# Last depth tile of a down projection with its low rank product in the same rows, in four weight versions

## What is computed

```python
def lora_add(base, inp, A, B):
    Ab = A[layer_idx][lora_indices]
    Bb = B[layer_idx][lora_indices]
    t = jnp.einsum('bri,bni->bnr', Ab, inp)
    return base + jnp.einsum('bor,bnr->bno', Bb, t) * SCALE
gate = lora_add(jnp.einsum('bnh,fh->bnf', x, W_gate), x, A_gate, B_gate)
up = lora_add(jnp.einsum('bnh,fh->bnf', x, W_up), x, A_up, B_up)
act = jax.nn.silu(gate) * up
down = lora_add(jnp.einsum('bnf,hf->bnh', act, W_down), act, A_down, B_down)
```

## Time and profile before

| | |
|---|---|
| median of 3 runs | 403.99 us (403.94 to 404.26) |
| profiled execution, its own time | 405.77 us |
| its span, first to last instruction | 403.9 us |
| PE busy | 398.2 us, 99% of the span, 1981 matmuls |
| weight loads (PEld, beside the matmuls) | 332.0 us, 82% |
| DVE busy | 309.1 us, 77% |
| ACT busy | 240.5 us, 60% |
| granted TensorE clock | 1.0 of full speed throughout |

### The profile page before, as it was taken

How to read it: one execution, slowest core, us unless ns; L and a number is a source line. 1 busy time by engine, 2 the same in 40 slices (tenths; PEclk the granted TensorE clock), 3 DMA queues, 4 the chain that set the end, 5 groups by cost and what they waited for, 6 DMA issues and landing times.

```text
span 403.9 us, 5691 instructions
## 1 busy us (share of the span) xinstructions
PE 398.2 (99%) x1981; PEld 332.0 (82%) x1981; DVE 309.1 (77%) x467; ACT 240.5 (60%) x381; POOL 13.4 (3%) x17
## 2 busy tenths in 40 slices
PE   8999999999999999999999999999999999999996
PEld 5899888888888888888888888888888888888885
DVE  4689978586745556683599887978787869899993
ACT  4769876767674379922655555565646485484740
POOL 5400000000000200000000000000000000000000
PEclk9999999999999999999999999999999999999999
DMA  7630234411111430300101113222131125105112
GB/s 260 199 115 2 79 105 111 119 52 54 52 54 32 133 99 0 105 0 0 54 0 52 54 53 104 63 94 97 60 104 54 60 83 194 54 0 197 53 52 104
DMA packets 14237, 31.88 MB, mean 79 GB/s; under 512 B 2306, under 2 KB 4610, under 8 KB 14210
## 3 DMA queue, kind: packets, MB, share of 16 engines
q1 hardware_dynamic: 13632, 29.96, 23.0%
q10 hardware_dynamic: 578, 1.57, 1.0%
HBM read 29.43 MB, written 2.10 MB: 78 GB/s over the span
## 4 chain that ended last, share of the span: by engine, by line
PE 97%; DMA 1%; issue 0%; DVE 0%; DVEq 0%; SPq 0%
PE bank L1311 47%; PE bank L1618 17%; PE bank L1502 15%; PE bank L1420 5%; PE bank L1448 3%; PE bank L1467 3%; PE bank L1456 3%; PE bank L1321 2%; PE bank L1516 1%; DMA wraw<-w_in 1%; PE bank L1523 0%; PE bank L1530 0%; DVE act L930 0%; DVEq L49 0%; SPq L287 0%
## 5 line engine op out<-in xcount | busy, mean ns | idle before, releaser
L1311 PE MATMUL bank<-xs,ws 128*128 128x512 f32 x840 | 194.2, 390 | 0.0
L1311 PEld LDWEIGHTS bank<-xs,ws 128*128 128x128 f32 x840 | 156.6, 188 | 32.3 <-ACT bank L399 0.5
L1502 PE MATMUL bank<-xs,wdc 128*128 128x512 f32 x264 | 61.5, 390 | 0.0
L1502 PEld LDWEIGHTS bank<-xs,wdc 128*128 128x128 f32 x264 | 49.1, 188 | 10.2 <-DVE xs L848 0.2
L399 ACT ACTIVATE xs<-act 128x512 fp32r<-128x512 f32 x71 | 42.9, 624 | 21.2 <-DVE act L995 7.6
L848 DVE TENSOR_TENSOR xs<-act,xs 128x512 fp32r<-128x512 f32 x71 | 47.7, 687 | 3.6 <-ACT xs L399 3.0
L848 DVE TENSOR_TENSOR ws<-wraw,ws 128x256 fp32r<-128x256 f32 (+2 forms) x49 | 32.5, 672 | 14.3 <-ACT ws L399 14.3
L399 ACT ACTIVATE bank<-bank 128x512 f32<-128x512 f32 x30 | 17.4, 580 | 39.8 <-PE bank L1311 38.9
L1618 PE MATMUL bank<-xs,vs 128*128 128x512 f32 x168 | 38.2, 389 | 0.0
L1618 PEld LDWEIGHTS bank<-xs,vs 128*128 128x128 f32 x168 | 31.5, 188 | 6.5
L399 ACT ACTIVATE ws<-wraw 128x256 fp32r<-128x256 f32 (+2 forms) x47 | 28.6, 619 | 11.1 <-PE bank L1311 4.1
(11 more groups left out here) (122 smaller groups left out, 423.1 us busy)
## 6 DMA issues: line engine op xcount, KB each, us to landing
wraw<-wgu_in SPq DMA_DIRECT2D x22, 512.0 KB, 3.3
wdr<-vs_in SPq DMA_DIRECT2D x7, 512.0 KB, 3.4
wdr<-wd_in SPq DMA_DIRECT2D x11, 256.0 KB, 2.6
wraw<-vj_in SPq DMA_DIRECT2D x3, 896.0 KB, 5.3
xa<-xT_in SPq DMA_DIRECT2D x4, 256.0 KB, 4.7
wraw<-w_in SPq DMA_DIRECT2D x4, 256.0 KB, 4.9
xa<-xT_in ACTq DMA_DIRECT2D x2, 512.0 KB, 6.2
bgu_raw<-bgu_in SPq DMA_DIRECT2D x32, 32.0 KB, 1.9
```

Of the source, the lines that this page charges most:

```text
L1311: ins = mm(z[:, :], ws[:, j % 2, w, s, k * P:(k + 1) * P], xs[:, c, r, k, :], start=(start and k == 0 and s == 0 and r == 0), stop=(k == 1 ...
L1502: ins = mm(z[:, :], wd[:, s, h * P:(h + 1) * P], x[r], start=(start and s == 0 and r == 0), stop=False, skip_group_check=True)
```

## The change

The 32 empty rows of the last depth tile are put to use. The result of `t_c` is scaled directly into rows 96 to 127 of the activation's last tile (`place_td`), and the weight tile gets B in the same rows. Since B depends on the sample and the 32 rows hold two samples' ranks, the weight tile exists in four versions, one for each pair of samples: 96 rows of W_down, the same in all four, and 32 rows of B. SP loads all four whole (`raw10`), ahead of tiles 6 to 9. `hi_w10` and `lo_w10` split them; version 0 lies in `wdc`, where the last tile was, the others in free parts of `ws`. `last_c(t, h)` takes the place of `main_c(t, 10)` and `lora_c(t, h)`: for each pair of 256 columns three passes. `tsum`, `bdr`, `td`, `bd` and their zeroing by GpSimd go. The ring slot of tile 10 isn't counted by `s_use` any more but by the fourth y.

```diff
-            tsum = sb("tsum", [32, 2, CH], f32, way)
-            bdr = sb("bdr", [64, 2, H], f32, way)
+            raw10 = sb("last_wd_raw", [P, 4, H], f32, way)
...
-        bd = [flat[:, 4 * CH:6 * CH].rearrange("p (q n) -> p q n", q=2) for flat in ws_flat]
-        td = [flat[:, 6 * CH:7 * CH] for flat in ws_flat]
+        w10 = [[wdc[:, FC - 1, s, :] for s in range(2)]] + [
+            [flat[:, (4 + s) * CH:(5 + s) * CH] for s in range(2)] for flat in ws_flat] + [[flat[:, 6 * CH:7 * CH] for flat in ws_flat]]
...
             sp.wait_ge(s_c12f, S1 // 2)
+            for v in range(4):
+                sp.dma_start(raw10[0:CR, v, :], wd_in[FC - 1, 0:CR, :]).then_inc(s_w10_ld, 16)
             for b in range(B):
-                row = 32 * (b // 4) + RANK * (b % 2)
-                sp.dma_start(bdr[row:row + RANK, b % 4 // 2, :],
-                             bd_in[ds(which[b], 1)].rearrange("o r h -> (o r) h")).then_inc(s_bd_ld, 16)
-            for n in range(6, FC):
+                row = CR + RANK * (b % 2)
+                sp.dma_start(raw10[row:row + RANK, b // 2, :],
+                             bd_in[ds(which[b], 1)].rearrange("o r h -> (o r) h")).then_inc(s_w10_ld, 16)
+            for n in range(6, FC - 1):
                 load_wd(n)
             load_w(G1 + 2)
...
-            pool.wait_ge(s_ad_pad, 1)
-            pool.wait_ge(s_p4, S1)
-            for t in range(2):
-                nc.gpsimd.memset(v32(bd[t][KS:P, :, :]), 0.0).then_inc(s_pad_d, 1)
-                nc.gpsimd.memset(v32(td[t][KS:P, :]), 0.0).then_inc(s_pad_d, 1)
...
-                    eng.wait_ge(s_act_pad, 1)
+                    eng.wait_ge(s_td, 4 * t + 4)
...
-                if u >= 10:
-                    a.wait_ge(s_use, u - 9)
+                if u == 20:
+                    a.wait_ge(s_y, 4)
+                elif u >= 10:
+                    a.wait_ge(s_use, min(u - 9, 11))
...
-            def hi_bd():
-                a.wait_ge(s_bd_ld, 16 * B)
+            def hi_w10(v):
+                a.wait_ge(s_w10_ld, 16 * (4 + B))
                 a.wait_ge(s_p4, S1)
-                for t in range(2):
-                    raw = bdr[32 * t:32 * t + 32, :, :]
-                    copy(bd[t][32 * t:32 * t + 32, :, :], raw).then_inc(s_bdhi, 1)
-                    copy(bd[t][64:KS, :, :], raw).then_inc(s_bdhi, 1)
-
-            def td_scale(t):
+                copy(w10[v][0], raw10[:, v, :]).then_inc(s_w10hi, 1)
+
+            def place_td(t):
                 a.wait_ge(s_t, t + 1)
                 for b in range(4):
-                    copy(tsum[:, t, b * P:(b + 1) * P], T_BANK[t][32 * b:32 * b + 32, b * P:(b + 1) * P], LORA_SCALE
-                         ).then_inc(s_tsum, 1)
-
-            def td_hi(t):
-                a.wait_ge(s_tsum, 4 * t + 4)
-                copy(td[t][0:32, :], tsum[:, t, :]).then_inc(s_tdhi, 1)
-                copy(td[t][32:64, :], tsum[:, t, :]).then_inc(s_tdhi, 1)
+                    first = t * CH + b * P
+                    copy(act[CR:P, FC - 1, first:first + P], T_BANK[t][32 * b:32 * b + 32, b * P:(b + 1) * P], LORA_SCALE
+                         ).then_inc(s_td, 1)
...
-                td_scale(t)
-                td_hi(t)
-            hi_wd(FC - 1)
+                place_td(t)
+            for v in range(4):
+                hi_w10(v)
             hi_ac(10)
-            hi_bd()
...
-            def lo_bd():
-                for t in range(2):
-                    v.wait_ge(s_bdhi, 2 * t + 1)
-                    sub(bd[t][32 - 32 * t:64 - 32 * t, :, :], bdr[32 * t:32 * t + 32, :, :], bd[t][32 * t:32 * t + 32, :, :]
-                        ).then_inc(s_bdlo, 1)
-
-            def td_lo(t):
-                v.wait_ge(s_tdhi, 2 * t + 1)
-                v.wait_ge(s_tsum, 4 * t + 4)
-                sub(td[t][64:KS, :], tsum[:, t, :], td[t][0:32, :]).then_inc(s_tdlo, 1)
+            def lo_w10(i):
+                v.wait_ge(s_w10hi, i + 1)
+                sub(w10[i][1], raw10[:, i, :], w10[i][0]).then_inc(s_w10lo, 1)
...
-            td_lo(0)
-            td_lo(1)
-            lo_wd(FC - 1)
+            for i in range(4):
+                lo_w10(i)
             lo_ac(10)
-            lo_bd()
...
-            def lora_c(t, h):
+            def last_c(t, h):
                 for q in range(2):
                     half = slice(256 * q, 256 * q + 256)
-                    ins = mm(Y_BANK[t][h][:, half], bd[t][:, q, h * P:(h + 1) * P], td[t][:, half],
-                             start=False, stop=(q == 1), skip_group_check=True)
+                    for s, r in PASSES:
+                        ins = mm(Y_BANK[t][h][:, half], w10[2 * t + q][s][:, h * P:(h + 1) * P], slot_c(11 * t + 10, r)[:, half],
+                                 start=False, stop=(s == 1), skip_group_check=True)
                 return ins
...
-            pe.wait_ge(s_wdlo, FC)
-            main_c(0, 10).then_inc(s_use, 1)
-            pe.wait_ge(s_bdhi, 4)
-            pe.wait_ge(s_bdlo, 2)
-            pe.wait_ge(s_pad_d, 4)
-            pe.wait_ge(s_tdhi, 4)
-            pe.wait_ge(s_tdlo, 2)
+            pe.wait_ge(s_w10lo, 4)
             for h in range(4):
-                lora_c(0, h).then_inc(s_y, 1)
-            pe.wait_ge(s_tsum, 8)
+                last_c(0, h).then_inc(s_y, 1)
+            pe.wait_ge(s_td, 8)
...
-                main_c(1, 10, range(h, h + 1))
-                lora_c(1, h).then_inc(s_y, 1)
+                last_c(1, h).then_inc(s_y, 1)
```

More of the change, by code:

```diff
@@ L192, in product_end @@
         def product_end(p):
-            return 12 + KF * (p + 1)
+            return 11 + KF * (p + 1)
         def tiles_of(g):
@@ L207, in build @@
         s_maskr = sem("mask_repeated")
-        s_act_pad, s_pad, s_pad_d = sem("short_act_padding_zero"), sem("padding_zero"), sem("down_lora_padding_zero")
+        s_act_pad, s_pad, s_ad_pad = sem("short_act_padding_zero"), sem("padding_zero"), sem("ad_padding_zero")
         s_table = sem("table_touched")
@@ L215, in build @@
         s_wd_ld = [sem("wd_loaded_even"), sem("wd_loaded_odd")]
-        s_ad_ld, s_bd_ld = sem("ad_loaded"), sem("bd_loaded")
+        s_ad_ld, s_w10_ld = sem("ad_loaded"), sem("last_wd_loaded")
         s_xr_ld = [sem(f"xres_loaded_{i}") for i in range(4)]
@@ L237, in build @@
         s_wdhi, s_wdlo = sem("wd_hi"), sem("wd_lo")
-        s_ad, s_ad_pad, s_bdhi, s_bdlo = sem("ad_placed"), sem("ad_padding_zero"), sem("bd_hi"), sem("bd_lo")
+        s_ad, s_w10hi, s_w10lo = sem("ad_placed"), sem("last_wd_hi"), sem("last_wd_lo")
         s_ahi, s_alo, s_use = sem("act_hi"), sem("act_lo"), sem("act_used")
-        s_t, s_tsum, s_tdhi, s_tdlo = (sem(n) for n in ("td_projected", "td_scaled", "td_hi", "td_lo"))
+        s_t, s_td = sem("td_projected"), sem("td_placed")
         s_y, s_sq, s_sqd, s_acc, s_sqhi, s_sqlo, s_ev, s_nm = (sem(n) for n in (
@@ L328, in _ @@
             load_w(G1 + 3)
-            sp.wait_ge(s_wdlo, FC)
+            sp.wait_ge(s_wdlo, FC - 1)
             sp.wait_ge(s_acc, 5)
@@ L575, in hi_down @@
                 if i >= 14:
-                    a.wait_ge(s_use, 12 + i - 13)
+                    a.wait_ge(s_use, 11 + i - 13)
                 elif i % 2 == 0:
@@ L639, in square @@
                 elif t == 1:
-                    a.wait_ge(s_wdlo, FC)
+                    a.wait_ge(s_wdlo, FC - 1)
                 to = third if (t, h) == (1, 2) else sqr[:, min(h, 1), :]
@@ L655, in rsqrt @@
                     a.wait_ge(s_warm, 3)
-                    a.wait_ge(s_bdlo, 2)
+                    a.wait_ge(s_w10lo, 4)
                 else:
@@ L1055, in norm @@
                 else:
-                    v.wait_ge(s_bdlo, 2)
-                    v.wait_ge(s_bdhi, 4)
+                    v.wait_ge(s_w10lo, 4)
                 nc.vector.scalar_tensor_tensor(y, N_BANK[t][:, :], H * NORM_EPS, root, ALU.add, ALU.mult).then_inc(s_var, 1)
```

## The result

The changed kernel took 403.16 us in the median of 22 runs (402.24 to 404.69), beside 404.49 us for the kernel before (403.73 to 407.13, 22 runs). The ratio is 0.9968 with a 95% interval of 0.9954 to 0.9982: 0.32% faster. The forecast was 402.5 us or 0.37% with a range of 402.1 to 403.1, so the sign and the size of the change were right and the time was outside the range by 0.06 us. The medians differ by 1.33 us. The profiled execution has a span of 400.5 us for 403.9 before, which is 3.4 us less and more than twice what was forecast. More than half of these 3.4 us lie outside the change, as the chains show. The miss of the time has to do with the base that the forecast started from.

What follows compares the result with a forecast made beforehand. TensorE (PE) was taken to bound the changed stretch without waits. 1.59 us of work leaving PE, less 0.1 us of waiting at the second half's closing, gave 1.5 us off 403.99: 402.5 us, range 402.1 to 403.1.

Steps and rivals of the forecast that it cites:

- the base that the forecast started from: Last step of the sum: takes 1.5 us off the unprofiled runs' median of 403.99 us, giving 402.5 us.
- three matmuls in a row that add into the same 256 columns: Rival in the new last tile: each second and third matmul waits for the one before, 5.2 us, 407.7 us; chance 0.03.

## What to carry to other kernels

Where an engine has no gap, count its instructions by their spacing in the chain, by shape, and the sum is good to a few hundredths of a microsecond; rows that are zeros in the last tile of a depth are room for any other product that adds to the same result. Slack that a change gives to a chain beside the critical one is worth something too, where that chain depends on transfers whose times vary: look for the place with the least slack and ask how often it is exceeded. When the profiled time and the median of the runs differ by more than the spread, find the stretch that makes the difference before choosing a base.

## What the runs showed of the hardware

The granted clock fell to 0.50 while PE waited for 6.7 us, and was back at 1.00 some 4 us after it resumed, at a cost of 2 us; waits of 0.7 to 1.0 us left it at 1.00. That the idle array is slowed and activity gives the clock back is what the Trainium skill says (TensorE: Matmul & The Clock Gate, "The HAM clock gate"), and the trace agrees. At the start of the program the recorded clock is 1.00 while four matmuls start in a microsecond for six later, so there it can't be used. A short wait of PE costs some 0.2 us more than its length: waits of 0.2 and 0.7 us made the stretch 0.40 and 0.91 us longer. And three matmuls in a row that add into the same 256 columns cost nothing extra, 119.6 ns each as with turns.
